# The product probs × 1/sum of the attention probabilities, moved from GpSimd to VectorE

## What is computed

```python
w = jnp.einsum('bhqd,bhkd->bhqk', q * scale, k * scale)
w = jax.nn.softmax(w.astype(jnp.float32), axis=-1).astype(q.dtype)
out = jnp.einsum('bhqk,bhkd->bhqd', w, v)
...
x = _layernorm(x + _L0_xattn_ref(ctx_1024, x, ...), axis=-1)
```

## Time and profile before

| What | Value |
|---|---|
| Time, median of 3 runs | 1647.21 us (1641.94 to 1647.63) |
| Span of the profiled execution | 1682.3 us |
| Softmax stage in it (83 to 1287 us) | 1204 us |
| VectorE busy, whole span | 1337.9 us, 80% |
| TensorE busy, whole span | 1437.9 us, 85% |
| GpSimd busy, whole span | 971.4 us, 58% |
| ScalarE busy, whole span | 973.4 us, 58% |
| Mean granted TensorE clock | 0.951 of full speed |

### The profile page before, as it was taken

One profiled execution on the slowest core, in us unless ns is written; L12 is line 12 of the kernel. 1 busy time (PEld: TensorE's weight loads), 2 busy tenths in 40 slices (PEclk: granted clock), 3 DMA queues, 4 the chain that ended last, 5 costly groups with the idle time before them and its releaser, 6 DMA issues.

```text
span 1682.3 us, 41166 instructions
## 1 busy us (share of the span) xinstructions
PE 1437.9 (85%) x10381; PEld 1230.8 (73%) x10381; DVE 1337.9 (80%) x5130; ACT 973.4 (58%) x3763; POOL 971.4 (58%) x1485
## 2 busy tenths in 40 slices
PE   4689999999999999999999999999997498988950
PEld 3478787877777777878777777778885498988840
DVE  4478988888888898888888888988876577766757
ACT  2266666666656665666666566666664255544535
POOL 2355665666666666666666666666644245544458
PEclk7599999999999999999999999999998699999975
DMA  3000000000000000000000000000000666766647
GB/s 82 11 11 7 14 18 15 15 14 13 15 15 15 15 13 13 17 14 15 13 15 13 15 14 15 13 15 16 8 11 15 189 217 208 223 191 199 203 132 214
DMA packets 89529, 95.40 MB, mean 57 GB/s; under 512 B 12137, under 2 KB 75756, under 8 KB 89282
## 3 DMA queue, kind: packets, MB, share of 16 engines
q1 hardware_dynamic: 69714, 71.97, 14.8%
q0 software_dynamic: 8896, 17.20, 3.0%
q10 hardware_dynamic: 10800, 5.06, 1.2%
HBM read 71.88 MB, written 23.35 MB: 57 GB/s over the span
## 4 chain that ended last, share of the span: by engine, by line
DVE 37%; issue 25%; ACT 15%; PE 15%; DMA 3%; another core or an unknown queue 2%; POOL 1%; DVEq 1%; SPq 1%; ACTq 0%; POOLq 0%
ACT probs L622 14%; DVE neg_max L767 7%; DVE pT L779 3%; PE ps_t L1419 3%; DVE k_pick L824 2%; DVE x1s L854 2%; PE ps_u L1419 2%; DVE turned L810 2%; DVE l_hat L871 2%; DVE yT L834 1%; PE ps_a L1381 1%; DVE top_atf L950 1%; DVE st_z L845 1%; DVE st_x L862 1%
## 5 line engine op out<-in xcount | busy, mean ns | idle before, releaser
L622 ACT ACTIVATE probs<-ps_s,neg_max 128x128 f32<-128x128 f32 x1024 | 362.6, 366 | 433.2 <-DVE neg_max L767 432.2
L508 POOL TENSOR_TENSOR probs_n<-probs,inv_sum 128x512 f32<-128x512 f32 x256 | 265.5, 1037 | 150.7 <-DVE inv_sum L773 148.6
L1265 PEld LDWEIGHTS ps_s<-kvT,u_sb 128*128 128x128 f32 x2048 | 255.3, 192 | 48.7 <-issue 44.9
L1265 PE MATMUL ps_s<-kvT,u_sb 128*128 128x128 f32 x2048 | 281.5, 281 | 3.2 <-issue 3.2
L1278 PE MATMUL ps_o<-value_w,tT 128*128 128x128 f32 x2048 | 261.8, 276 | 2.7 <-ACT tT L633 2.2
L1298 PE MATMUL ps_t<-pT,kv_rows 128*128 128x512 f32 x512 | 262.3, 594 | 0.8 <-DVE pT L779 0.8
L1278 PEld LDWEIGHTS ps_o<-value_w,tT 128*128 128x128 f32 x2048 | 244.7, 192 | 6.8 <-ACT tT L633 4.1
L570 POOL DMA_INDIRECT y_rows<-wvT,f_id x144 | 146.4, 1017 | 169.9 <-DVE wvT L1179 124.9
L520 POOL DMA_INDIRECT x_rows<-routed,pos_i x128 | 136.3, 1065 | 132.0 <-DVE pos_i L1003 100.3
L1313 PE MATMUL ps_u<-lT_hi,score_hi 128*128 128x256 f32 x512 | 184.5, 360 | 27.4 <-DVE lT_lo L893 21.1
L622 ACT ACTIVATION_READ_ACCUMULATOR probs<-ps_s,neg_max 128x1 f32 x1024 | 207.6, 203 | 0.0
(11 more groups left out here) (246 smaller groups left out, 3453.2 us busy)
## 6 DMA issues: line engine op xcount, KB each, us to landing
u_sb<-in_expert_w SPq DMA_DIRECT2D x45, 578.0 KB
tT<-in_expert_w SPq DMA_DIRECT2D x27, 578.0 KB
f_x<-x_rows SPq DMA_DIRECT2D x72, 130.0 KB
tT<-y_rows SPq DMA_DIRECT2D x32, 256.0 KB, 3.7
x_raw<-in_x SPq DMA_DIRECT2D x64, 64.0 KB, 1.8
c_raw<-in_ctx_in SPq DMA_DIRECT2D x128, 32.0 KB, 2.0
out<-u_sb ACTq DMA_DIRECT2D x16, 256.0 KB, 3.0
y_rows<-wvT,f_id POOLq DMA_INDIRECT x144
```

The costliest lines, as they stand in the source:

```text
L508: nc.gpsimd.tensor_tensor(probs_n[:, sl], probs[:, sl], inv_sum[:, sl, :].rearrange("p (u o) -> p u o", o=1).to_broadcast([P, UP, P]), ALU ...
L622: last = nc.scalar.activation(probs[:, sl, j], ps_s[sl][:, j * P:(j + 1) * P], ACT.Exp, bias=neg_max[:, sl, j:j + 1], accum_out=sums[:, sl ...
L1265: last = nc.tensor.matmul(ps_s[sl][:, j * P:(j + 1) * P], u_sb[:, c // 2, BT * p + b, h:h + 2].rearrange("p h s -> p (h s)"), kvT[:, c, 1 ...
```

## The change

`scale` leaves GpSimd's program. The same product of 128x512 is written on VectorE, in `inverse_sum`, directly behind the reciprocal: it waits for the reciprocal's own semaphore and, as `scale` did, for the transposes of the unit before the last (the slot of `probs_n`). It raises the same semaphore `p_done` that TensorE and ScalarE wait for. Nothing else moves; TensorE's and ScalarE's orders are the same.

```diff
--- before.py
+++ after.py
@@ -501,15 +501,6 @@
                 pool.wait_ge(eps_done, j + 1)
                 nc.gpsimd.tensor_tensor(rs, ve, m_half[:, 0:rs.shape[-1]], ALU.pow).then_inc(rstd_done, 1)
 
-            def scale(t, k):
-                n, sl = t * 4 + k, k % 2
-                pool.wait_ge(inv_done, n + 1)
-                pool.wait_ge(pT_ps, count(n - 1))
-                nc.gpsimd.tensor_tensor(
-                    probs_n[:, sl], probs[:, sl],
-                    inv_sum[:, sl, :].rearrange("p (u o) -> p u o", o=1).to_broadcast([P, UP, P]),
-                    ALU.mult).then_inc(p_done, 1)
-
             def route(j, q, sl):
 
                 pool.wait_ge(rows_kept, j + 1)
@@ -528,9 +519,6 @@
                 for k in range(UNITS):
                     if k == 0 and on(t, -2):
                         rstd(mv_z2[:, p, 1:2], ve_z2[:, p], rs_z2[:, p], eps_ln, z2_moments, t - 1, z2_eps, z2_rstd, t - 2)
-                    if on(t, 0):
-                        scale(t, k)
-
                     if k == 0 and on(up, 3):
                         rstd(mv_in[:, p3, :, 1], ve_in[:, p3], rs_in[:, p3], eps_ln, in_moments, 2 * up + 8, in_eps, in_rstd, up + 3)
                     if k == 0 and on(up, 2):
@@ -771,6 +759,12 @@
                     n, sl = t * 4 + k, k % 2
                     dve.wait_ge(exp_done, n + 1)
                     nc.vector.reciprocal(inv_sum[:, sl], sums[:, sl]).then_inc(inv_done, 1)
+                    dve.wait_ge(inv_done, n + 1)
+                    dve.wait_ge(pT_ps, count(n - 1))
+                    nc.vector.tensor_tensor(
+                        probs_n[:, sl], probs[:, sl],
+                        inv_sum[:, sl, :].rearrange("p (u o) -> p u o", o=1).to_broadcast([P, UP, P]),
+                        ALU.mult).then_inc(p_done, 1)
 
                 def keep_pT(k):
                     m, ss = t * 4 + (k - 1), (k - 1) % 2
```

## The result

| | before | after |
|---|---|---|
| Time, median | 1647.4 us (1641.9 to 1648.0) | 1735.0 us (1729.9 to 1738.9) |
| Span of the profiled execution | 1682.3 us | 1733.6 us |
| First to last reciprocal of the softmax | 1199.6 us | 1283.9 us |
| From there to the end | 397.9 us | 364.5 us |
| Distance between two periods in the loop, its four periods in turn | 18.6, 18.6, 21.1 and 18.6 us | 20.1, 20.0, 22.3 and 19.8 us |

A forecast was written before the change was run, and what follows sets the result against it. The prediction took the softmax stage to be bound by a VectorE-ScalarE loop through `neg_max`. A price of 184 us less a relief of 106 us gave +78 us on 1647.2, so 1725 us, range 1695 to 1765.

The forecast's parts named there:

- What bounds the kernel: Softmax stage: a loop between VectorE and ScalarE, which waits for `neg_max` before 255 of 256 exponential groups, 432.2 us.
- The price: Product on VectorE between reciprocal and copy of `pT`: 0.72 us more per unit, 184 us in all, on the path.
- The relief: VectorE steps no longer held up by GpSimd's product: 1.77 us gained per period, 106 us in all.
- All four steps: `routed`, `x1s`, `l_hat`, `k_pick` on VectorE, held until GpSimd's product ends; gains of 0.48, 0.36, 0.36 and 0.57 us.
- The sum: Price 184 us less relief 106 us: 78 us slower, some 1.2 us on a period of 18.8.
- rival 1: The new product on VectorE is held up by GpSimd's small powers in units 0 and 3: 26 us more, 1751; chance 0.09.
- Rival 2: Hold-ups stay in part through other long GpSimd instructions; half the relief lost is 53 us more, 1778; chance 0.07.
- Rivals 3 and 4: `neg_max` doesn't release the exponentials, 33 us faster, 1614; or TensorE sets the pace, no change, 1647; chance 0.03 each.
- rival 4: TensorE, busy in 93% of the softmax stage, sets the pace and its gaps absorb the change: 1647; chance 0.03.

The follow-up runs named there:

- behind_copy: The kernel after, with the product on VectorE placed behind the copy of `pT` instead of ahead of it; 1717.1 us.
- no_product: The kernel after without the product on either engine, the softmax division left out and TensorE transposing the exponentials themselves; 1590.6 us.
- extra_reduce: The kernel before, product kept on GpSimd, with one more 128x512 PSUM reduction on VectorE ahead of the copy of `pT`; 1717.3 us.
- before_again: The kernel before, unchanged, profiled a second time; span 1645.1 us.
- after_filler: The kernel after with six extra identity transposes per period on TensorE, ahead of its wait for `kv_prod`; 1730.9 us.
- steps_ahead: The kernel before, with `route_rows`, `x1_norm` and `latent_norm` written ahead of the reciprocals of units 0, 1 and 2; 1612.2 us.
- pick_on_act: As steps_ahead, with `k_pick` taken from VectorE and made by ScalarE behind the exponentials of unit 3; 1610.3 us.
- both_ahead: The kernel after (product on VectorE) with the same steps ahead of the reciprocals as in steps_ahead; 1670.0 us.

## Why the prediction was right

It named 1725 us in 1695 to 1765, slower; measured 1735.

**What bounds the kernel: held.** ScalarE waits for `neg_max` 256 times of 256, and the idle time before the reciprocals did not take any of the new work (110.5 us for 110.9).

**The price, 0.72 us per unit: held.** The product takes 692 ns, the duration of the row taken for it, with no extra for the stretched operand; the copy starts 0.83 us behind the reciprocal instead of 0.10, which is 0.73. That 0.12 of it is dependency was tried by itself (behind_copy, 0.54 per period for 4 x 0.12).

**The relief, 1.77 us per period: held.** All four steps have their short durations, and `top_atf`, which another GpSimd step holds up, has kept its 0.43. The distances between reciprocals are 5.04, 4.76, 4.17 and 5.79 us: longer by 0.23, 0.38, 0.37 and 0.17, 1.16 in all before rounding. The steps of the prediction give 0.24, 0.36, 0.36 and 0.15, 1.11 in all. no_product and extra_reduce showed that this was a hold-up on the path, and not only shorter records.

**The sum, +78 us: 10 too small.** 63 distances between periods with 1.16 us more are 73 us; the stage grew by 84, and the rest of the run by 3.5 (364.5 us for 361.0 in before_again). In the stage two things that the prediction has no term for make up the difference. VectorE has two short stalls in every pass of the loop, 13 times 0.39 us ahead of line 839, where no wait ends, and 13 times 0.25 us ahead of a product: 8.4 us by the waits shown above. Every kernel of the series with the product on VectorE has the 13 of 0.39 us, after_filler among them, so they don't hang on TensorE's clock. The kernel before and no_product have no such stall. But extra_reduce, with the product on GpSimd, has it one instruction later (13 times 0.46 us for 0.10), and steps_ahead has 14 of some 0.26 us ahead of a copy of `pT`: they don't hang on the product as such. What causes them was not tried. The rest is TensorE's clock, some 3 to 6 us by the sum and by after_filler against after. "TensorE and ScalarE only get more slack" is the sentence of the prediction that missed this: slack of TensorE had a price.

**The range: an error in its high end.** It is written as 1725 + 26 + 14, for rival 1 and a quarter of the relief; a quarter of 106 us is 26 or 27, which would have put the end near 1778. It decides nothing, since 1735 lies well below either.

**Rival 1, the new product is held up itself: out here.** Its durations are 691 to 694 ns in all 256 instances, those of unit 3, where GpSimd's `rs_qk` is running, among them. By the Trainium skill (SBUF — State Buffer, Who interferes with whom) an instruction with two SBUF inputs contends with a GpSimd one that reads SBUF; that rule, the traces bear out where GpSimd's instruction is the product of 512 columns (line 840 in steps_ahead, `kv_prod` in pick_on_act) or a step of 128x128 (the product itself in both_ahead, unit 2), and not where it is a power on 1 or 2 columns. So the rival was out because in this order of steps no 128x128 step of GpSimd runs beside the product; with `l_hat` moved, as in both_ahead, its mechanism is there. **Rival 2, hold-ups that stay: out.** **Rivals 3 and 4, faster or the same: out**, by the wait for `neg_max`; but no_product and steps_ahead show how near rival 4's bound was: with 1 us per period less on VectorE, TensorE is the bound.

## What to carry to other kernels

Work that moves from a helper engine to the one that sets the pace costs its full start-to-start time there, and what it gives back has to be looked for in the neighbours: the same instruction with two durations, the long one ending with the helper's instruction, is time that comes back when the helper stops, or when the two are moved 0.6 us apart. Moving apart was the better of the two here (1612 us for 1735), but the hold-up passes to whichever instruction of its kind comes next, so the whole stretch beside the helper's instruction would have to be filled with steps that it doesn't touch (no run here did that). A moved step can also bring the helper's next work forward into a new overlap, as `l_hat` did in both_ahead. Give the unprofiled median more weight than one profiled execution when a stage that the change leaves alone differs between two profiles.

## What the runs showed of the hardware

**The hold-up works both ways.** In the kernel after, GpSimd's sum of 2 columns `ve_in` starts while the product runs on VectorE (duration ns min/median/max):

```profile
L500 POOL TENSOR_TENSOR ve_in<-mv_in,eps_ln x64: 192/632/656, 18.6 to 1271.9; 128x2 f32<-128x2 f32 x64
```

Its median was 312 ns before. It costs next to nothing there: VectorE waited 0.2 us in the whole run for `rs_in`, which GpSimd makes from it. In both_ahead GpSimd's `c_scaled` of 128x128 goes from 454 to 993 ns in the median beside the product.

**TensorE's clock fell behind short waits.** Granted clock (last but two of the columns) in two stretches of the kernel after, around the end of a pass of the loop:

```profile
872.00:876.00 4.00, 3.27 (x21) 2.16 (x19) 3.97 (x19) 3.31 (x13) 2.65 (x6) 1.00 0.00 0
878.50:881.70 3.20, 3.20 (x11) 2.17 (x10) 2.43 (x12) 1.99 (x9) 1.97 (x4) 0.50 0.06 21
```

It is at 0.50 (1.2 GHz of 2.4) from 878.5 on; before that, TensorE had waited 0.61 us for ScalarE's `u_sb` and then 1.03 us for `kv_prod`, at 877.1. Each of the eleven such stretches of the kernel after begins right behind its wait for `kv_prod`, and so do those of behind_copy (28, with waits of mostly 0.65 and 0.88 us) and of extra_reduce (23, mostly 0.61 and 0.87). The kernel before has waits for `kv_prod` of 0.85 us in the same place, but waits for `u_sb` in only 4 periods, and the full clock all through this stage. In both_ahead the clock fell 12 times behind a wait for `kv_prod` of 0.94 us with no more than 0.2 us for `u_sb` before it. In the slow stretches TensorE falls behind, and VectorE waits for its scores or transposes. Why some periods with the same waits lose the clock and others not is open. Six small transposes per period, whose results nobody reads, were enough to keep it, and worth 18 us in behind_copy and some 4 in after, the latter not clear of the scatter.
